# A batched graph layer: sums of two batches turned in one go, the last two products halved, and batches 1 and 2 split into high and low parts like the later ones

## Chip, cores and metric

The kernel runs on one core of one Trainium2 chip. The metric is the device time of one execution in microseconds (us). Before the change three runs took 205.3, 205.43 and 205.56 us, median 205.43. The profiled execution took 205.48 us; its span, from the first to the last instruction, is 203.7 us.

## What is computed

For each of 16 batches with 512 nodes and 128 features:

```
h    = relu(layernorm(x))                         # 512 x 128
A    = [adj, adj, S, adj^T, adj^T, S^T, I]        # 7 relations; S is I shifted by one row
HW_r = h @ W[r, :128] + W_edges[r] @ W[r, 128:]   # the second term is one row per relation
out  = x + max over r of (A_r @ HW_r) + b
```

The relations with adj and adj^T (two each) need `adj @ h` and `adj^T @ h`, called g and gT here, and the row sums of adj and adj^T for the edge term. The other three work on h itself.

## The kernel before, in words

Everything is kept transposed, 128 features by 512 nodes. The batches go through one after another, numbered 0 to 15, in a pipeline over the engines. The order on each engine is written out by hand, and semaphores tie the engines together. There is no planner.

TensorE (PE) does for a batch: `aggregate_T` (bank_gT = gT), `turn_h` (four transposes of h), `aggregate` (bank_g), `turn_sums` (four 128x128 products that turn the row sums into rows, `bank_s`), products 0 to 2 on hT, `begin_products` (four 32-row products that start the banks of products 3 to 6 with the edge term from `c_rows` and `sumsT`), and products 3 to 6 on gT and g. A product is three passes (L870 to L872), since numbers are kept as a high part in fp32r and a low part that holds the rest: high by high, low by high, high by low. From batch 2 (`FIRST`) on, the aggregations take such parts too: `a_hi`, `a_lo` of adj, `aT_hi`, `aT_lo` of its transpose, `h_hi`, `h_lo` of h, four chunks of 128 nodes each, so 12 matmuls per aggregation. Batches 0 and 1 are aggregated whole, in plain fp32 (L763, L770, L780, L789), and batch 2 half and half.

ScalarE (ACT) makes the high parts with the row sums as a by-product (`split_adj` L422, `split_adjT` L431; for batches 0 and 1 it forms the sums alone, L403, L411, L505, L512), the standard deviation (`std_of` L395), h and h_hi (`make_h` L443, L449), the high parts of hT, gT and g (L455, L461, L467), `sumsT` (L473), and starts the running maximum with product 0 (`begin_best` L480).

VectorE (DVE) makes mean and variance (`variance` L550, L557), turns them into scale and shift (`scale_and_shift` L587, L589), makes the low parts of the first two chunks (`split_adj_lo` L596, `split_adjT_lo` L603) and of h, hT, gT, g, and takes the maximum over products 1 to 6 (`take_best` L637, L640).

GpSimd (POOL) makes the low parts of the last two chunks (L334, L341), spreads the sums into `sum_parts` (`part_sums` L307, L311), starts the DMA that adds x onto the bias (`add_bias` L319), and adds it to the maximum (`finish` L327). SyncE (SP) issues the loads and stores (L231 adj, L244 adjT, L250 bias, L254 store, L289 last store).

Which work depends on which, around the change: h of batch b+1 needs scale and shift, these need `std_of`, which needs `variance`. Product 0 of a batch needs the low part of hT, so it waits for ACT (L455), then DVE (L614). The last product of batch 15 is computed in two halves of 256 nodes, each with its own bank, maximum, sum and store.

Of the kernel before, what the change touches and what calls it, by code (L numbers as in the profile page):

```python
# [11 lines left out]
P = 128  # L12
# [14 lines left out]
FIRST = 2  # L27
NX = 4


def gnn_kernel(nc: bass.Bass, x: bass.AP, xT: bass.AP, adj: bass.AP, adjT: bass.AP, W: bass.AP,
# [14 lines left out]
    with ExitStack() as ctx:  # L46
# [26 lines left out]
        summed = pair("summed", [P, 2, C, N], mybir.dt.bfloat16)  # L73
# [5 lines left out]
        g_lo = sb("g_lo", [P, N], F32R)  # L79

# [43 lines left out]
        last_banks = (bank_g, bank_p[0])  # L124
# [66 lines left out]
        best_done = sem("best_done")  # L191
        xb_in = [sem(f"xb_in{i}") for i in range(2)]
# [15 lines left out]

        block = ctx.enter_context(nc.Block())

        @block.sync
        def _(sp):
# [7 lines left out]
            def load_adj(b):  # L220
                q = b % 2
                if b >= 2:
                    if b - 2 < FIRST:
                        sp.wait_ge(sums_ready, 2 * (b - 2) + 1)
# [4 lines left out]
                if b > 2 + FIRST:  # L229
                    sp.wait_ge(alo_last_ready, (b - 2 - FIRST) * NG)  # L230
                sp.dma_start(adj_sb[q][:, :, :], adj_dram[b]).then_inc(adj_in[q], 16)  # L231

            def load_adjT(b):
                q = b % 2
                if b >= 2:
                    if b - 2 < FIRST:
                        sp.wait_ge(sums_ready, 2 * (b - 2) + 2)
# [30 lines left out]
            sp.dma_start(w_sb[:, 5:7, :], w_dram[:, 0:2, :]).then_inc(wa_in, 16)  # L268
            load_adj(1)
            load_adjT(1)  # L270
            load_x(2)
            load_bias(0)
            load_x(3)
            load_adj(2)
            load_adjT(2)
            load_bias(1)
            for b in range(1, B):
                if b + 3 < B:
                    load_x(b + 3)
# [15 lines left out]
        def _(pool):  # L295
            def part_sums(b):
                q = b % 2
# [6 lines left out]
                if b >= 2:  # L304
                    pool.wait_ge(sumsT_psum, b - 1)
                for copy in range(2):
                    last = nc.gpsimd.tensor_copy(sum_parts[q][:, :, :, :, 2 * copy], s)  # L307
                last.then_inc(parts_hi, 1)
                pool.wait_ge(parts_hi, b + 1)
                for copy in range(2):  # L310
                    last = nc.gpsimd.tensor_tensor(sum_parts[q][:, :, :, :, 2 * copy + 1], s,  # L311
                                                   sum_parts[q][:, :, :, :, 2 * copy].bitcast(F32), ALU.subtract)
# [57 lines left out]
            add_bias(0)  # L370
            part_sums(1)
            finish(0)
            add_bias(1)
            part_sums(2)
            add_bias(2)
            for b in range(2, B):

                pool.wait_ge(aTlo_ready, (b - FIRST + 1) * ND)
                finish(b - 1)
                if b + 1 < B:  # L380

# [4 lines left out]
                    part_sums(b + 1)  # L386
                    add_bias(b + 1)

        @block.scalar
        def _(act):  # L390
# [8 lines left out]
            def sum_adj(b):  # L399
                q = b % 2  # L400
                act.wait_ge(adj_in[q], times(b))
                for c in range(C):
                    last = nc.scalar.activation(summed[q][:, 0, c, :], adj_sb[q][:, c, :], ACT.Copy,  # L403
                                                accum_out=sums[q][:, 0, c:c + 1])
                last.then_inc(sums_ready, 1)

            def sum_adjT(b):
                q = b % 2
                act.wait_ge(adjT_in[q], times(b))
                for c in range(C):  # L410
                    last = nc.scalar.activation(summed[q][:, 1, c, :], adjT_sb[q][:, c, :], ACT.Copy,  # L411
                                                accum_out=sums[q][:, 1, c:c + 1])
                last.then_inc(sums_ready, 1)

            def split_adj(b):
# [4 lines left out]
                act.wait_ge(parts_lo, b - 1)  # L420
                for c in range(C):
# [12 lines left out]
            def make_h(b):  # L434
# [10 lines left out]
                last.then_inc(h_ready, 1)  # L445
                if b < FIRST:
                    return
                act.wait_ge(h_ready, b + 1)
# [20 lines left out]
            def copy_sumsT(b):  # L469
                act.wait_ge(sumsT_psum, b + 1)  # L470
# [32 lines left out]
            for c in range(C):  # L503
                act.wait_ge(adj0_in[c], 16)
                last = nc.scalar.activation(summed[0][:, 0, c, :], adj_sb[0][:, c, :], ACT.Copy,  # L505
# [4 lines left out]
            for c in range(C):  # L510
                act.wait_ge(adjT0_in[c], 16)
                last = nc.scalar.activation(summed[0][:, 1, c, :], adjT_sb[0][:, c, :], ACT.Copy,  # L512
# [4 lines left out]
            make_h(1)  # L517
            copy_sumsT(0)
            act.wait_ge(ccol_ready, 1)
            begin_best(0)  # L520
            sum_adj(1)
            std_of(2)
            sum_adjT(1)
            for b in range(1, B):

                if 2 <= b < B - 1:
                    split_adj(b + 1)
                split_gT(b)
# [15 lines left out]
        def _(dve):  # L544
# [82 lines left out]
            def take_best(b, i):  # L627
                q = b % 2
                r = ORDER[i]
                if i == 1:  # L630
                    dve.wait_ge(best_begun, b + 1)
                else:
                    dve.wait_ge(best_done, b * NBEST + i - 1)
                dve.wait_ge(prod_psum, b * NPROD + i + 1)
                product = bank_of[i][:, 0:N]
# [10 lines left out]
            nc.vector.tensor_reduce(row_hi[:, :], groups[:, :, 0:2], AXIS.XY, ALU.add)  # L646
            nc.vector.tensor_reduce(row_lo[:, :], groups[:, :, 2:4], AXIS.XY, ALU.add).then_inc(masks_ready, 1)
# [15 lines left out]
            for i, rels in enumerate((A_RELS, AT_RELS)):  # L663
# [29 lines left out]
            scale_and_shift(2)

            split_gT_lo(1)
            split_hT_lo(1)
            split_h_lo(2)
            split_g_lo(1)
            variance(3)
            take_best(1, 1)  # L700
            take_best(1, 2)
            split_adj_lo(2)
            scale_and_shift(3)
            for i in range(NH, NPROD):
                take_best(1, i)

            for b in range(2, B):
                if b + 2 < B:
                    variance(b + 2)
                split_adjT_lo(b)  # L710
                split_gT_lo(b)
                split_hT_lo(b)
                if b + 2 < B:
                    scale_and_shift(b + 2)
                if b + 1 < B:
                    split_adj_lo(b + 1)
# [8 lines left out]
            dve.wait_ge(best_done, B * NBEST - 1)  # L725
            for i, nodes in enumerate(HALVES):
                dve.wait_ge(prod_psum, B * NPROD + i)
                nc.vector.tensor_tensor(best[q][:, nodes], last_banks[i][:, nodes], best[q][:, nodes],
                                        ALU.max).then_inc(best_done, 1)
                dve.wait_ge(best_done, B * NBEST + i)  # L730
                nc.vector.tensor_tensor(o_sb[q][:, nodes], best[q][:, nodes], x_bias[q][:, nodes],
                                        ALU.add).then_inc(last_out_ready, 1)

        @block.tensor
        def _(pe):
# [8 lines left out]
            def turn_sums(b):  # L744
                pe.wait_ge(parts_lo, b + 1)
                if b >= 1:
                    pe.wait_ge(best_done, (b - 1) * NBEST + 2)
                for c in range(C):
                    last = nc.tensor.matmul(bank_s[:, c * P:(c + 1) * P],  # L749
                                            sum_parts[b % 2][:, c, :, :, :].rearrange("p d g k -> p (d g k)"),  # L750
# [212 lines left out]
```

## Time and profile before

| | us |
|---|---|
| time of three runs, median | 205.43 |
| time of the profiled execution | 205.48 |
| its span | 203.7 |
| PE busy | 197.7 (97%) |
| VectorE busy | 170.0 (83%) |
| ScalarE busy | 160.1 (79%) |
| GpSimd busy | 115.8 (57%) |

The time of the execution is 1.8 us above its span, which is start and end outside the instructions. The chain that ended last is made of the pieces of work that each released the next; where one engine makes up nearly all of it, the others only count where they make that engine wait. A line such as `50.09 1.64 ACT L443 ACTIVATE h<-x_sb x4` says that four instructions of line 443 ran from 50.09 us for 1.64 us; a bracket behind it says how long the engine was idle before and what ended that.

### The profile page before, as it was taken

The numbers are of one execution on the slowest core, as the hardware profiler recorded it, in microseconds if no ns is written. First come the engines' busy times: TensorE is split into PE (matmuls) and PEld (weight loads), VectorE is DVE, ScalarE is ACT, GpSimd is POOL, SyncE is SP. The second block draws the span as 40 slices with busy tenths as digits, with TensorE's granted clock in tenths as the row PEclk, the third lists the DMA queues.
The fourth block names the chain that finished last, engine by engine and source line by source line (L and its number), as shares of the span: only waits on it lengthen the run. The fifth ranks groups of instructions, "written<-read, shape, count | busy, mean of one in ns | idle before, by whom it ended". The sixth has DMA issues, their size and how long they took to land.

```text
span 203.7 us, 3448 instructions
## 1 busy us (share of the span) xinstructions
PE 197.7 (97%) x918; PEld 151.2 (74%) x918; DVE 170.0 (83%) x411; ACT 160.1 (79%) x432; POOL 115.8 (57%) x162
## 2 busy tenths in 40 slices
PE   6999999999999999999999999999999999999991
PEld 6456466778787787878778787878878787887871
DVE  3487969989898998989989898998989899878565
ACT  3887989996969879696988969697896969795230
POOL 4041341477574938657592956759295675939500
PEclk9999999999999999999999999999999999999999
DMA  5999999997888979789987969799795969570501
GB/s 161 333 356 358 373 346 273 293 357 191 258 315 232 350 183 342 201 269 306 292 304 162 381 153 333 228 246 357 198 395 107 312 199 343 208 154 0 100 4 51
DMA packets 33748, 51.07 MB, mean 251 GB/s; under 512 B 1873, under 2 KB 11329, under 8 KB 33729
## 3 DMA queue, kind: packets, MB, share of 16 engines
q1 hardware_dynamic: 31152, 46.53, 67.1%
q0 software_dynamic: 2304, 4.20, 13.3%
q8 instruction: 7, 0.11, 0.2%
q10 hardware_dynamic: 272, 0.13, 0.2%
q14 instruction: 13, 0.10, 0.1%
HBM read 46.65 MB, written 4.19 MB: 250 GB/s over the span
## 4 chain that ended last, share of the span: by engine, by line
PE 94%; DMA 2%; DVE 2%; SPq 0%; issue 0%; DVEq 0%
PE bank_p L870 13%; PE bank_p L871 11%; PE bank_p L872 10%; PE bank_g L832 6%; PE bank_g L835 6%; PE bank_g L841 6%; PE bank_gT L818 6%; PE bank_gT L812 6%; PE bank_gT L808 6%; PE bank_p L741 3%; PE bank_p L860 3%; PE bank_p L749 3%; DMA adj_sb<-in_adj_dram 2%; PE bank_g L789 2%; PE bank_gT L780 2%; PE bank_g L770 2%
## 5 line engine op out<-in xcount | busy, mean ns | idle before, releaser
L334 POOL TENSOR_TENSOR a_lo<-adj_sb,a_hi 128x512 fp32r<-128x512 f32 x26 | 33.1, 1296 | 31.6 <-DVE a_lo L596 28.5
L640 DVE TENSOR_TENSOR best<-bank_p,best 128x512 f32<-128x512 f32 x48 | 33.1, 691 | 7.2 <-PE bank_p L872 6.0
L422 ACT ACTIVATE a_hi<-adj_sb 128x512 fp32r<-128x512 f32 x56 | 34.5, 620 | 1.3 <-DMA adj_sb<-in_adj_dram 1.3
L431 ACT ACTIVATE aT_hi<-adjT_sb 128x512 fp32r<-128x512 f32 x56 | 34.4, 620 | 0.0
L341 POOL TENSOR_TENSOR aT_lo<-adjT_sb,aT_hi 128x512 fp32r<-128x512 f32 x26 | 33.2, 1297 | 0.9 <-ACT aT_hi L431 0.3
L327 POOL TENSOR_TENSOR o_sb<-best,x_bias 128x512 f32<-128x512 f32 x15 | 19.8, 1317 | 19.1 <-DVE aT_lo L603 15.9
L637 DVE SCALAR_TENSOR_TENSOR best<-bank_p,c_col,best 128x512 f32<-128x512 f32 x32 | 24.0, 750 | 6.6 <-ACT best L480 6.0
L461 ACT ACTIVATE gT_hi<-bank_gT 128x512 fp32r<-128x512 f32 x16 | 9.5, 595 | 25.0 <-PE bank_gT L818 24.7
L443 ACT ACTIVATE h<-x_sb,shift,rstd 128x128 f32<-128x128 f32 x60 | 24.7, 488 | 0.0
L870 PE MATMUL bank_p<-hT_hi,w_hi 128*128 128x512 f32 x48 | 20.0, 417 | 0.0
L872 PE MATMUL bank_p<-hT_lo,w_hi 128*128 128x512 f32 x48 | 18.7, 390 | 0.0
L871 PE MATMUL bank_p<-hT_hi,w_lo 128*128 128x512 f32 x48 | 18.7, 389 | 0.0
L596 DVE TENSOR_TENSOR a_lo<-adj_sb,a_hi 128x512 fp32r<-128x512 f32 x28 | 18.0, 683 | 0.0
L603 DVE TENSOR_TENSOR aT_lo<-adjT_sb,aT_hi 128x512 fp32r<-128x512 f32 x28 | 17.9, 681 | 0.0
L319 POOL DMA_DIRECT2D x_bias<-in_xT_dram x16 | 13.8, 863 | 5.0 <-DMA x_bias<-in_biasT_dram 4.6
L832 PE MATMUL bank_g<-aT_hi,h_hi 128*128 128x512 f32 x54 | 16.3, 422 | 0.0
L808 PE MATMUL bank_gT<-a_hi,h_hi 128*128 128x512 f32 x54 | 14.9, 397 | 0.0
L835 PE MATMUL bank_g<-aT_hi,h_lo 128*128 128x512 f32 x54 | 14.7, 392 | 0.0
L841 PE MATMUL bank_g<-aT_lo,h_hi 128*128 128x512 f32 x54 | 14.6, 390 | 0.0
L818 PE MATMUL bank_gT<-a_lo,h_hi 128*128 128x512 f32 x54 | 14.6, 390 | 0.0
L812 PE MATMUL bank_gT<-a_hi,h_lo 128*128 128x512 f32 x54 | 14.5, 389 | 0.0
L619 DVE TENSOR_TENSOR gT_lo<-bank_gT,gT_hi 128x512 fp32r<-128x512 f32 x16 | 11.1, 691 | 3.8 <-ACT gT_hi L461 2.8
(122 smaller groups left out, 477.7 us busy)
## 6 DMA issues: line engine op xcount, KB each, us to landing
adj_sb<-in_adj_dram SPq DMA_DIRECT2D x15, 1024.0 KB, 7.5
adjT_sb<-in_adjT_dram SPq DMA_DIRECT2D x15, 1024.0 KB, 8.3
x_bias<-in_biasT_dram SPq DMA_DIRECT2D x16, 256.0 KB, 6.5
x_bias<-in_xT_dram POOLq DMA_DIRECT2D x16, 256.0 KB, 4.1
x_sb<-in_x_dram SPq DMA_DIRECT2D x15, 256.0 KB, 8.3
out_dram<-o_sb SPq DMA_DIRECT2D x15, 256.0 KB, 5.5
adj_sb<-in_adj_dram SPq DMA_DIRECT2D x4, 256.0 KB, 5.1
adjT_sb<-in_adjT_dram SPq DMA_DIRECT2D x4, 256.0 KB, 5.1
```

The costliest lines, as they stand in the source:

```text
L334: nc.gpsimd.tensor_tensor(a_lo[q][:, c, :], adj_sb[q][:, c, :], a_hi[q][:, c, :].bitcast(F32), ALU.subtract).then_inc(alo_last_ready, 1)
L341: nc.gpsimd.tensor_tensor(aT_lo[q][:, c, :], adjT_sb[q][:, c, :], aT_hi[q][:, c, :].bitcast(F32), ALU.subtract).then_inc(aTlo_last_ready, 1)
L422: nc.scalar.activation(a_hi[q][:, c, :], adj_sb[q][:, c, :], ACT.Copy, accum_out=sums[q][:, 0, c:c + 1]).then_inc(ahi_ready, 1)
L431: nc.scalar.activation(aT_hi[q][:, c, :], adjT_sb[q][:, c, :], ACT.Copy, accum_out=sums[q][:, 1, c:c + 1]).then_inc(aThi_ready, 1)
L640: op = nc.vector.tensor_tensor(best[q][:, :], product, best[q][:, :], ALU.max)
L808: nc.tensor.matmul(bank_gT[:, 0:N], h_hi[q][:, c, :], a_hi[q][:, c, :], start=(c == 0 and b > FIRST), stop=False)
L818: last = nc.tensor.matmul(bank_gT[:, 0:N], h_hi[q][:, c, :], a_lo[q][:, c, :], start=False, stop=(c == split_chunks(b)[-1]))
L832: nc.tensor.matmul(bank_g[:, 0:N], h_hi[q][:, c, :], aT_hi[q][:, c, :], start=(c == 0 and b > FIRST), stop=False)
L835: nc.tensor.matmul(bank_g[:, 0:N], h_lo[q][:, c, :], aT_hi[q][:, c, :], start=False, stop=False)
L870: nc.tensor.matmul(dst, w_hi[:, i, :], hi[:, nodes], start=start, stop=False)
L871: nc.tensor.matmul(dst, w_lo[:, i, :], hi[:, nodes], start=False, stop=False)
L872: return nc.tensor.matmul(dst, w_hi[:, i, :], lo[:, nodes], start=False, stop=stop)
```

## The change

In batches 4 to 15 the row sums of two neighbours go through one `turn_sums` and one `copy_sumsT`. The even one of a pair (`leads`) does it, with the sums of the odd one (`follows`) in other columns of the same `sum_parts`, and `c_rows` has a second set of rows that picks them. For that, ACT splits all of the odd batch's adj and adjT before it takes gT of the even one, and SP loads adjT ahead of the store. The last two products of batch 15, not one, are halved, and POOL adds x and bias of the first half. `FIRST` is 1: batch 1 is split like the later ones and batch 2 in all chunks. The first bias is loaded ahead of adj of batch 1, the second ahead of adj of batch 2. The order on ACT, DVE and POOL for batches 0 to 4 is written out anew.

```diff
-FIRST = 2
+FIRST = 1
+PAIRED = 4
+        def leads(b):
+            return b >= PAIRED and (b - PAIRED) % 2 == 0 and b + 1 < B
+        def follows(b):
+            return b >= 1 and leads(b - 1)
+        def turn_of(b):
+            return b if b < PAIRED else PAIRED + (b - PAIRED) // 2
...
+            load_bias(0)
             load_adj(1)
             load_adjT(1)
             load_x(2)
-            load_bias(0)
+            load_bias(1)
+            load_adj(2)
             load_x(3)
-            load_adj(2)
             load_adjT(2)
-            load_bias(1)
...
                 if b + 2 < B:
                     load_adj(b + 2)
+                    load_adjT(b + 2)
                 store(b - 1)
...
             add_bias(0)
+            pool.wait_ge(alo_ready, ND)
+            pool.wait_ge(hlo_ready, 1)
+            split_adj_last(1)
             part_sums(1)
+            pool.wait_ge(aTlo_ready, ND)
+            split_adjT_last(1)
+            add_bias(1)
             finish(0)
...
                 finish(b - 1)
+                if leads(b):
+                    part_sums(b + 1)
                 if b + 1 < B:
                     pool.wait_ge(alo_ready, (b - FIRST + 2) * ND)
                     pool.wait_ge(hlo_ready, b - FIRST + 2)
                     split_adj_last(b + 1)
                     split_adjT_last(b + 1)
-                    part_sums(b + 1)
+                    if not leads(b):
+                        part_sums(b + 1)
...
-            sum_adj(1)
+            split_adj(1)
+            split_adjT(1)
...
+            begin_best(2)
+            std_of(3)
+            make_h(3)
+            split_h(3)
+            split_adjT(3)
+            std_of(4)
+            for b in range(3, B):
+                if b < B - 1:
                     split_adj(b + 1)
+                if leads(b):
+                    split_adjT(b + 1)
                 split_gT(b)
                 split_hT(b)
...
+            for i in range(NH, NPROD):
+                take_best(2, i, i - 1)
+            variance(4)
+            scale_and_shift(4)
+            for b in range(3, B):
+                split_adjT_lo(b)
...
                 aggregate_T(b)
                 turn_h(b)
                 aggregate(b)
-                turn_sums(b)
+                if not follows(b):
+                    turn_sums(b)
...
-            for nodes, to in zip(HALVES, last_banks):
-                product(B - 1, NPROD - 1, nodes, to)
+            for i in range(2):
+                for k in range(NLAST):
+                    product(B - 1, NPROD - NLAST + k, HALVES[i], last_banks[k][i])
```

On ACT, before the change, this stands from `begin_best` of batch 2 (it writes best0) to `h` of batch 4 (h0, std0 and rstd0 again belong to an even batch, a_hi0 too).

```order
L480 ACTIVATE best0<-bank_p0,c_col 128x512
L431 ACTIVATE aT_hi1,sums1<-adjT_sb1 128x512 x4
L422 ACTIVATE a_hi0,sums0<-adj_sb0 128x512 x4
L461 ACTIVATE gT_hi<-bank_gT 128x512
L455 ACTIVATE hT_hi<-bank_p1 128x512
L395 ACTIVATE std1<-mean_var1,eps 128x4
L443 ACTIVATE h0<-x_sb0,shift0,rstd0 128x128 x4
```

On ACT, with the change, from `begin_best` of batch 2 to `h` of batch 4:

```order
L500 ACTIVATE best0<-bank_p0,c_col 128x512
L427 ACTIVATE std1<-mean_var1,eps 128x4
L460 ACTIVATE h1<-x_sb3,shift1,rstd1 128x128 x4
L469 ACTIVATE h_hi1<-h1 128x512
L448 ACTIVATE aT_hi1,sums1<-adjT_sb1 128x512 x4
L427 ACTIVATE std0<-mean_var0,eps 128x4
L439 ACTIVATE a_hi0,sums0<-adj_sb0 128x512 x4
L481 ACTIVATE gT_hi<-bank_gT 128x512
L475 ACTIVATE hT_hi<-bank_p1 128x512
L460 ACTIVATE h0<-x_sb0,shift0,rstd0 128x128 x4
```

The standard deviation of batch 4 (std0, L427) now stands ahead of the splitting of adj of batch 4 and of gT and hT of batch 3. Before, the one for batch 4 (std0, L395) came after gT and hT of batch 2, and h of batch 3 was made there, ahead of `begin_best` of batch 2.

On DVE, with the change, from the scale of batch 3 (rstd1) to the low part of hT of batch 3; best0 is the maximum of batch 2, mean_var0 and rstd0 are of batch 4:

```order
L635 SCALAR_TENSOR_TENSOR shift1<-mean_var1,rstd1 128x4
L642 TENSOR_TENSOR a_lo1<-adj_sb1,a_hi1 128x512 x2
L695 SCALAR_TENSOR_TENSOR best0<-bank_p1,c_col,best0 128x512
L695 SCALAR_TENSOR_TENSOR best0<-bank_p2,c_col,best0 128x512
L655 TENSOR_TENSOR h_lo1<-h1,h_hi1 128x512
L698 TENSOR_TENSOR best0<-bank_p3,best0 128x512
L698 TENSOR_TENSOR best0<-bank_p4,best0 128x512
L698 TENSOR_TENSOR best0<-bank_p5,best0 128x512
L698 TENSOR_TENSOR best0<-bank_g,best0 128x512
L596 BN_STATS stats<-x_sb0 128x6 x4
L601 MEMSET wait_carrier 128x1
L603 BN_AGGR mean_var0<-stats 128x2 x4
```

On DVE, before the change, the same stretch, from the scale of batch 3 (rstd1, shift1, which stands in the middle of the maxima of batch 1) on:

```order
L589 SCALAR_TENSOR_TENSOR shift1<-mean_var1,rstd1 128x4
L640 TENSOR_TENSOR best1<-bank_p3,best1 128x512
L640 TENSOR_TENSOR best1<-bank_p4,best1 128x512
L640 TENSOR_TENSOR best1<-bank_p5,best1 128x512
L640 TENSOR_TENSOR best1<-bank_g,best1 128x512
L550 BN_STATS stats<-x_sb0 128x6 x4
L555 MEMSET wait_carrier 128x1
L557 BN_AGGR mean_var0<-stats 128x2 x4
L603 TENSOR_TENSOR aT_lo0<-adjT_sb0,aT_hi0 128x512 x2
```

The mean and variance of batch 4 stood behind the maxima of batch 1; they now stand behind those of batch 2, and the scale of batch 3 behind g of batch 2.

## Rows read from the trace of the kernel before

**Rows 1.** The chain that ended last, shares of the span by engine.
```profile
PE 94%; DMA 2%; DVE 2%; SPq 0%; issue 0%; DVEq 0%
```
**Rows 2.** Stretches of batches 1, 2, 3: busy per engine, granted clock, DMA share, GB/s.
```profile
19.98:33.67 13.69, 13.67 (x51) 8.16 (x51) 11.20 (x36) 12.56 (x37) 3.88 (x7) 1.00 1.05 332
33.67:46.17 12.50, 12.50 (x54) 8.66 (x54) 11.76 (x28) 12.47 (x36) 7.31 (x10) 1.00 1.04 327
46.17:57.97 11.80, 11.80 (x59) 9.40 (x58) 10.63 (x26) 9.85 (x28) 8.12 (x11) 1.00 0.84 249
```
**Rows 3.** Chain in order of time: start, us, piece; batches 1 and 3.
```profile
27.75 0.40 PE bank_p L749 x4
...
48.90 0.44 PE bank_p L741 x4
...
52.10 0.40 PE bank_p L749 x4
52.50 0.29 PE bank_p L870
...
54.60 0.43 PE bank_p L860 x3
```
**Rows 4.** Timeline of ACT, batches 0, 1 and 3.
```profile
17.24 0.60 ACT L473 ACTIVATE sumsT<-bank_p 128x512 fp32r<-128x512 f32 x1 [1.02 <-PE bank_p L749]
...
18.30 0.63 ACT L403 ACTIVATE summed<-adj_sb 128x512 bf16<-128x512 f32 x1
...
48.93 0.60 ACT L461 ACTIVATE gT_hi<-bank_gT 128x512 fp32r<-128x512 f32 x1 [1.87 <-PE bank_gT L818]
...
49.90 0.30 ACT L395 ACTIVATE std<-mean_var,eps 128x4 f32<-128x4 f32 x1
50.09 1.64 ACT L443 ACTIVATE h<-x_sb,shift,rstd 128x128 f32<-128x128 f32 x4
...
52.31 0.58 ACT L467 ACTIVATE g_hi<-bank_g 128x512 fp32r<-128x512 f32 x1
...
53.28 0.69 ACT L480 ACTIVATE best<-bank_p,c_col 128x512 f32<-128x512 f32 x1
```
**Rows 5.** Costliest groups: busy, mean ns of one; the splitting of adj on ACT.
```profile
L422 ACT ACTIVATE a_hi<-adj_sb 128x512 fp32r<-128x512 f32 x56 | 34.5, 620 | 1.3 <-DMA adj_sb<-in_adj_dram 1.3
```
**Rows 6.** Timeline of DVE, batches 0 and 3.
```profile
18.45 1.54 DVE L637 SCALAR_TENSOR_TENSOR best<-bank_p,c_col,best 128x512 f32<-128x512 f32 x2 [1.38 <-ACT best L480]
...
47.01 0.86 DVE L550 BATCH_NORM_STATS2 stats<-x_sb 128x6 f32<-128x128 f32 x4
...
48.01 0.28 DVE L557 BATCH_NORM_AGGREGATE mean_var<-stats 128x2 f32<-128x6 f32 x3
...
50.77 0.17 DVE L587 RECIPROCAL rstd<-std 128x4 f32<-128x4 f32 x1
...
51.05 1.28 DVE L596 TENSOR_TENSOR a_lo<-adj_sb,a_hi 128x512 fp32r<-128x512 f32 x2
52.43 0.69 DVE L609 TENSOR_TENSOR h_lo<-h,h_hi 128x512 fp32r<-128x512 f32 x1
...
56.03 2.14 DVE L640 TENSOR_TENSOR best<-bank_p,best 128x512 f32<-128x512 f32 x3 [0.47 <-PE bank_p L872]
```
**Rows 7.** Timeline of POOL, batches 0 and 3.
```profile
20.60 1.00 POOL L319 DMA_DIRECT2D x_bias<-in_xT_dram  x1 [4.60 <-DMA x_bias<-in_biasT_dram]
...
53.26 2.55 POOL L334 TENSOR_TENSOR a_lo<-adj_sb,a_hi 128x512 fp32r<-128x512 f32 x2 [2.40 <-DVE a_lo L596]
```
**Rows 8.** One line, the loads of adjT (L244): landing times.
```profile
DMA to landing us min/median/max: 6.6/8.3/12.3
```
**Rows 9.** Timeline of DVE at the end, batch 15.
```profile
197.52 2.14 DVE L640 TENSOR_TENSOR best<-bank_p,best 128x512 f32<-128x512 f32 x3 [0.48 <-PE bank_p L872]
199.86 0.42 DVE L728 TENSOR_TENSOR best<-bank_g,best 128x256 f32<-128x256 f32 x1 [0.20 <-DVE best L640]
...
201.11 0.42 DVE L731 TENSOR_TENSOR o_sb<-best,x_bias 128x256 f32<-128x256 f32 x1
```

More of the change, by code:

```diff
@@ L20 @@
 NBEST = NPROD - 1
+NLAST = 2
 NH = len(H_RELS)
@@ L303, in part_sums @@
                     pool.wait_ge(aThi_ready, (b - FIRST + 1) * NS)
-                if b >= 2:
-                    pool.wait_ge(sumsT_psum, b - 1)
+                if turn >= 2:
+                    pool.wait_ge(sumsT_psum, turn - 1)
+                parts = sum_parts[turn % 2]
                 for copy in range(2):
-                    last = nc.gpsimd.tensor_copy(sum_parts[q][:, :, :, :, 2 * copy], s)
+                    last = nc.gpsimd.tensor_copy(parts[:, :, :, :, first + 2 * copy], s)
                 last.then_inc(parts_hi, 1)
@@ L310, in part_sums @@
                 for copy in range(2):
-                    last = nc.gpsimd.tensor_tensor(sum_parts[q][:, :, :, :, 2 * copy + 1], s,
-                                                   sum_parts[q][:, :, :, :, 2 * copy].bitcast(F32), ALU.subtract)
+                    last = nc.gpsimd.tensor_tensor(parts[:, :, :, :, first + 2 * copy + 1], s,
+                                                   parts[:, :, :, :, first + 2 * copy].bitcast(F32), ALU.subtract)
                 last.then_inc(parts_lo, 1)
@@ L396, in std_of, with split_adj @@
                                      bias=eps[:, :]).then_inc(std_ready, 1)
[L399 to L415, printed above, removed]
+            def split_adj(b, chunks=range(C)):
                 q = b % 2
@@ L419, in split_adj @@
                     act.wait_ge(gT_psum, b - 1)
-                act.wait_ge(parts_lo, b - 1)
-                for c in range(C):
+                if b >= 2:
+                    act.wait_ge(parts_lo, b - 1)
+                for c in chunks:
                     nc.scalar.activation(a_hi[q][:, c, :], adj_sb[q][:, c, :], ACT.Copy,
@@ L645, in _ @@
             groups = ident[:, :].rearrange("p (g s) -> p g s", s=GROUP)
-            nc.vector.tensor_reduce(row_hi[:, :], groups[:, :, 0:2], AXIS.XY, ALU.add)
-            nc.vector.tensor_reduce(row_lo[:, :], groups[:, :, 2:4], AXIS.XY, ALU.add).then_inc(masks_ready, 1)
+            for s in range(2):
+                nc.vector.tensor_reduce(row_hi[:, s:s + 1], groups[:, :, 4 * s:4 * s + 2], AXIS.XY, ALU.add)
+                last = nc.vector.tensor_reduce(row_lo[:, s:s + 1], groups[:, :, 4 * s + 2:4 * s + 4], AXIS.XY, ALU.add)
+            last.then_inc(masks_ready, 1)
             first_variance(0, half_stats_done, half_aggr_done)
@@ L709, in _ @@
+            variance(4)
+            scale_and_shift(4)
+            for b in range(3, B):
+                split_adjT_lo(b)
+                if 3 < b < B - 2:
                     variance(b + 2)
-                split_adjT_lo(b)
                 split_gT_lo(b)
                 split_hT_lo(b)
+                if b == 3:
+                    variance(b + 2)
+                if b + 1 < B:
+                    split_adj_lo(b + 1)
+                    if not leads(b):
+                        split_h_lo(b + 1)
+                split_g_lo(b)
+                if leads(b):
+                    split_h_lo(b + 1)
+                for i in range(1, NPROD - NLAST * int(b == B - 1)):
+                    take_best(b, i, i - 1)
@@ L918, in _ @@
             for b in range(1, B):
-                if b < FIRST:
-                    aggregate_T_whole(b)
-                else:
-                    aggregate_T(b)
+                aggregate_T(b)
                 turn_h(b)
-                if b < FIRST:
-                    aggregate_whole(b)
-                else:
-                    aggregate(b)
-                turn_sums(b)
+                aggregate(b)
+                if not follows(b):
+                    turn_sums(b)
                 for i in range(NH):
```

267 lines of the change are left out of this document (138 added, 129 removed).

## Prediction

> **What bounds the kernel now.** I read the chain of waits first: PE makes up 94% of it [rows 1], so only time that PE works or is made to wait counts. Then the stretches batch by batch: batch 1, aggregated whole in fp32, takes 13.69 us, batch 2, half whole, 12.50, batch 3 and every later one 11.8; PE is busy in all but 0.02 us of each, at a granted clock of 1.00 [rows 2]. DVE is busy 10.63 us of 11.80, ACT 9.85: PE bounds, with little room on DVE. The chain in order of time gives the parts of a batch. In batch 3, which begins at 46.17, `aggregate_T` ends at 48.90, `turn_sums` runs from 52.10 to 52.50, product 0 starts at 52.50 (6.33 us into the batch), products 0 to 2 last to 54.60, and the edge terms with products 3 to 6 to 57.97 (3.37 us) [rows 2, 3].
>
> **The change part by part.** All sums are made against the profiled execution, 205.48 us, 0.05 above the median of the runs.
>
> *Batches 1 and 2 split.* Ideally they shrink to 11.8 us, by 1.9 and 0.7. Batch 1 does not get its share, for its parts come late. ACT begins to split adj of batch 1 where it now forms its sums, at 18.30, and a chunk takes 0.62, so the second is ready at 19.6 [rows 4, 5]. DVE takes the first maximum from 18.45 (0.77), then two low parts of adj (1.2) and of h (0.7): done at 21.05 [rows 6]. Only then POOL starts its two chunks, 0.14 later (as after h_lo, 52.43 + 0.69 to 53.26), and ends 2.55 later, at 23.7 [rows 6, 7]. PE, ready for the last one at 22.7, ends `aggregate_T` at about 24.1. The same in `aggregate`: DVE takes three more maxima (0.77 + 2 x 0.72) and two low parts, to 24.4, POOL needs 2.55 more, to 27.05, PE ends at about 27.4. Now it ends at 27.75 [rows 3]. So batch 1 gains 0.3, not 1.9. In batch 2 the same sums put each low part 0.5 us or more ahead of its use, and it takes 11.8: another 0.7. Batch 3 then starts at 45.2 instead of 46.17. POOL can begin that early because the first bias is loaded sooner: it now waits 4.60 us for it, to 20.60 [rows 7]. With 256 KB ahead of it, adj of batch 1 lands later, but nothing waited for it at 18.30. The copy of h to h_hi that batch 1 gains hides in the 1.02 us that ACT waits ahead of sumsT [rows 4].
>
> *The new order around batch 3.* This is the costly edit. `std_of(4)` now stands on ACT ahead of the split of adj of batch 4 and of gT and hT of batch 3, and what it waits for, the variance of batch 4, stands on DVE behind the maxima of batch 2. Counted from the start of batch 2 (durations start to start from [rows 4 to 6]): ACT takes gT_hi at 2.76 (48.93 less 46.17), hT_hi, then splits adj of batch 3 (2.45) to 6.2, makes g_hi and sumsT (0.97) and `begin_best` (0.6), to 7.7, and std of batch 3, to 8.0. DVE: scale 0.28, two low parts 1.2, maxima 1 and 2 1.5, h_lo 0.65, maxima 3 to 6 4 x 0.72, variance 1.28: it ends at 15.7, which is 3.9 us into batch 3. Then std (0.3, of which 0.2 before the next can start), split of adj of batch 4 (2.45), gT_hi and hT_hi (0.5 + 0.6) on ACT: 19.4; hT_lo behind gT_lo on DVE: 20.2. Product 0 of batch 3 starts at 20.3, where it would have started at 11.8 + 6.33 = 18.1: PE waits 2.2 us. Behind hT_hi ACT still has h and h_hi of batch 4 (2.2), g_hi (0.5) and sumsT (0.6), to 22.6; product 2, ready at 21.7, waits 0.95 more. On DVE the variance of batch 5, two low parts, h_lo and g_lo (1.2 + 1.2 + 0.6 + 0.7) follow hT_lo and end at 23.85; the edge terms, ready at 23.4, wait 0.55. Sum: 3.7 us. Batch 4 starts 27.4 us after batch 2, at 60.7; before, at 57.97. The two early gains, 1.0, are paid back 3.7-fold. The waits are sure in place and uncertain in size: if PE meets each with 0.1 to 0.2 more delay on resuming, 4.2; if DVE overlaps better than start to start, 3.0.
>
> *Pairs.* Batches 5, 7, 9, 11, 13, 15 lose `turn_sums`: 0.40 us, and perhaps the 0.06 by which the first pass behind it is longer than a usual 0.23 (0.29) [rows 3]. I take 0.43, six times 2.6; bounds 2.4 and 2.8. The six copies of sumsT that ACT drops are off the path. What the pair adds is lateness: ACT splits adj and adjT of the odd batch (4.9 us) ahead of gT_hi of the even one, behind adjT of the even one, and reaches gT_hi 3.5 us into the batch, not 2.76. hT_lo is then ready at 5.4 and needed at 6.33; POOL's parts of the odd batch's sums are ready at 4.6 and needed at 5.9; g_lo at 7.3, needed at 8.4. So the cover is 0.9 us, and behind that each tenth of lateness costs PE a tenth per pair.
>
> *The end.* Since DVE bounds it, the maxima count: now three whole ones from 197.52, then two half maxima and two half sums, the last ending at 201.53, 4.01 us [rows 9]. With the change two whole ones (1.44), then half maxima of products 5 and 6, twice, and one half sum; POOL adds the other. With 0.45 for a half that waits for the one before and 0.34 for one that doesn't, this is 1.45 + 0.45 + 0.34 + 0.45 + 0.45 + 0.42 = 3.56: 0.45 less. POOL's half sum, estimated at half of its 1.3 us, ends at 3.1, before DVE's.
>
> Sum: -0.3 - 0.7 + 3.7 - 2.6 - 0.45 = -0.35; with PE's slower resuming I take -0.3, so 205.2 us.
>
> **The rivals.**
> 1. *The wait in batch 3 doesn't come, or half of it.* For it: DVE has idle time, and the maxima of batch 2 end about 1 us into batch 3 today (47.01 starts the variance) [rows 6]. Against it: DVE can't start them before std of batch 3, which is behind `begin_best`. Without the 3.7, the time is 201.5; with half, 203.3.
> 2. *The load of the odd adjT is late (slower).* It is issued when POOL has made the low parts of the odd batch before, about 13.5 us into a pair, and ACT wants it at 24.2: 10.7 us. Landing took 8.3 us in the median and 12.3 at worst [rows 8]. From 11.6 us on the 0.9 us of cover is gone; at 12.3, 1.6 us late, hT_lo costs PE 0.8 us in five pairs: 205.2 + 4 = 209.2. Against it: the long landings fall in the first 30 us, where the DMA share is above 1.00, and 0.84 is usual later [rows 2].
> 3. *DVE becomes the bound in the odd batches.* It works 10.63 us [rows 2] and waits 0.47 for product 3 [rows 6]; at 11.4 us a batch some 0.3 is left. If it doesn't go below 11.8, the pairs bring nothing: 207.8.
> 4. *PE's clock falls in the wait of batch 3.* The granted clock is 1.00, the level of 2.4 GHz, in every stretch above, where PE never pauses [rows 2]; no row shows it after a pause of 2.2 us. The 5.5 us of products left in batch 3 at half the clock, 1.2 GHz, less 1.5 of waiting that they would hide, add 4: 209.2. [...]
>
> **How the numbers follow.** Forecast 62%, 205.2, its own range 204.4 to 206.2; rival 1 23% (half of that below 203); rival 2 7%; rival 3 5%; rival 4 3%. A measurement of this kernel can tell 0.2%, 0.41 us, from no change. The forecast lies 0.23 below the median, within that bound: of its 62% I give 24 to faster (below 205.02), 28 to the same, 10 to slower (above 205.84). With rival 1 faster has 47%, the same 28%, and slower, with rivals 2 to 4, 25%. The range, 202.9 to 206.8, leaves out the lower half of rival 1 and most of rivals 2 to 4.
>
> **What would show it.** Right: batch 3 lasts 15 to 16 us, with PE waiting ahead of product 0 for hT_lo, and ACT idle about 2.5 us ahead of the std of batch 4, released by the variance; batch 1 some 13.4; later even batches 11.8, odd ones 11.4; no `turn_sums` in these. Wrong: batch 4 starting before 58 us (rival 1), gT_hi of even batches released by adjT's DMA (rival 2), odd batches of 11.8 with maxima as the last to end (rival 3), a granted clock below 1.00 in batch 3 (rival 4).

## The result and the profile after

The changed kernel takes 209.13 us (median of four runs, 208.81 to 209.53), the kernel before in the same comparison 205.50: a ratio of 1.0168, 95% interval 1.0143 to 1.0193. It is slower by about 3.5 us, where 205.2 was forecast and 206.8 was the upper end of the range. The profiled execution took 208.81 us, its span is 207.0, 3.3 above that of before. Ratios leave out runs over 1.5% above the fastest of the same kernel (one of e4 below, two of e8, 206.3 to 207.5 us); medians keep them.

The stretches of batches 1 to 5 answer to [rows 2] (from, to, length, busy time and count of PE, PEld, DVE, ACT, POOL, then granted clock, DMA share, GB/s):

```profile
19.96:34.24 14.28, 12.80 (x61) 9.32 (x58) 12.76 (x28) 12.08 (x34) 10.80 (x12) 1.00 1.08 346
34.24:46.95 12.71, 12.36 (x59) 9.35 (x57) 11.65 (x27) 10.23 (x28) 6.88 (x9) 1.00 0.90 293
46.95:62.72 15.77, 14.42 (x59) 10.49 (x58) 13.82 (x37) 13.29 (x40) 13.00 (x14) 0.89 0.77 234
62.72:75.15 12.43, 12.04 (x59) 9.32 (x57) 10.70 (x26) 10.68 (x31) 9.54 (x14) 1.00 0.84 253
75.15:86.50 11.35, 11.35 (x55) 8.95 (x54) 10.77 (x26) 8.32 (x23) 7.89 (x8) 1.00 0.87 263
```

PE, busy all the time before, now waits in batches 1 to 4 and 12. The six odd batches from 5 on are 0.44 us shorter each, as forecast; batch 3 is 3.97 longer (forecast 3.7). By the first matmul of each batch, batch 2 starts at 34.24 instead of 33.51 and batch 3 at 46.95 instead of 46.01 (the stretches of [rows 2] are cut 0.16 later). So batch 1 costs 0.7 more where 0.3 less was forecast, batch 2 0.2 more where 0.7 less was, and batches 4 and 12, forecast unchanged, are longer by 0.64 and 0.45. PE's timeline names the main waits (not shown are 0.71 us for POOL's a_lo in batch 1, which was forecast, and 0.35 for DVE's aT_lo in batch 3):

```profile
28.04 0.49 PE L892 MATMUL bank_g<-aT_lo,h_hi 128*128 128x512 f32 x1 [0.74 <-POOL aT_lo L355]
...
38.21 1.20 PE L884 MATMUL bank_g<-aT_hi,h_hi 128*128 128x512 f32 x4 [0.23 <-DVE best L698]
...
55.61 0.73 PE L922 MATMUL bank_p<-hT_hi,w_hi 128*128 128x512 f32 x1 [0.83 <-issue]
...
69.17 0.66 PE L833 MATMUL bank_p<-ident_r,sum_parts 128*128 128x128 f32 x4 [0.39 <-POOL sum_parts L325]
...
162.20 0.66 PE L833 MATMUL bank_p<-ident_r,sum_parts 128*128 128x128 f32 x4 [0.20 <-POOL sum_parts L325]
```

Three of the five lead to POOL. The wait of batch 3 that is put down to "issue" ends right behind DVE's hT_lo (55.51), as predicted. On ACT, too, batch 3 looks as predicted: std of batch 4 waits 2.45 us for the variance, and gT_hi starts 6.67 us into the batch, where it started 2.92 into it before (48.93 less 46.01). DVE's line first, then two of ACT:

```profile
54.83 0.68 DVE L660 TENSOR_TENSOR hT_lo<-bank_p,hT_hi 128x512 fp32r<-128x512 f32 x1
```
```profile
50.96 0.30 ACT L427 ACTIVATE std<-mean_var,eps 128x4 f32<-128x4 f32 x1 [2.45 <-DVE mean_var L603]
...
53.62 0.58 ACT L481 ACTIVATE gT_hi<-bank_gT 128x512 fp32r<-128x512 f32 x1
```

How long POOL and DVE took in batches 1 and 2 was in no step of the prediction. First POOL, then DVE (start, duration of the group):

```profile
21.20 2.54 POOL L348 TENSOR_TENSOR a_lo<-adj_sb,a_hi 128x512 fp32r<-128x512 f32 x2 [4.23 <-DVE h_lo L655]
23.69 1.27 POOL L321 CAST sum_parts<-sums 128x16 fp32r<-128x16 f32 x2
25.05 0.45 POOL L325 TENSOR_TENSOR sum_parts<-sums,sum_parts 128x16 fp32r<-128x16 f32 x2
25.44 2.55 POOL L355 TENSOR_TENSOR aT_lo<-adjT_sb,aT_hi 128x512 fp32r<-128x512 f32 x2
...
32.27 2.56 POOL L348 TENSOR_TENSOR a_lo<-adj_sb,a_hi 128x512 fp32r<-128x512 f32 x2 [2.16 <-DVE a_lo L642]
```
```profile
23.08 1.81 DVE L649 TENSOR_TENSOR aT_lo<-adjT_sb,aT_hi 128x512 fp32r<-128x512 f32 x2
24.82 1.41 DVE L698 TENSOR_TENSOR best<-bank_p,best 128x512 f32<-128x512 f32 x2
...
33.56 1.82 DVE L655 TENSOR_TENSOR h_lo<-h,h_hi 128x512 fp32r<-128x512 f32 x1
```

Where POOL works and DVE has an operation with two inputs in SBUF, one or both get long: DVE's aT_lo 1.81 us for two, where a_lo of the same size took 1.28, h_lo 1.82 instead of 0.69 [rows 6], POOL's CAST 1.27 for two instead of 0.34 (the line of e2 below). A maximum, which reads one input from PSUM, keeps its 0.7. The delay shows as duration of the instruction, not as idle time with a releaser.

### The profile page after: what moved, and what is told of

The parts are those of the page before. It is cut to its first block and busy times, and to the rows that moved or that the text cites. A ratio compares the mean times of both kernels' runs of the same rounds, so it can differ in the third digit from the quotient of the medians.

```text
span 207.0 us, 3419 instructions
## 1 busy us (share of the span) xinstructions
PE 196.9 (95%) x910; PEld 151.1 (73%) x910; DVE 177.5 (86%) x420; ACT 157.5 (76%) x427; POOL 134.7 (65%) x171
## 5 line engine op out<-in xcount | busy, mean ns | idle before, releaser
L348 POOL TENSOR_TENSOR a_lo<-adj_sb,a_hi 128x512 fp32r<-128x512 f32 x30 | 38.3, 1298 | 46.2 <-DVE a_lo L642 19.4
L355 POOL TENSOR_TENSOR aT_lo<-adjT_sb,aT_hi 128x512 fp32r<-128x512 f32 x30 | 38.3, 1300 | 0.4 <-ACT aT_hi L448 0.4
L439 ACT ACTIVATE a_hi<-adj_sb 128x512 fp32r<-128x512 f32 x60 | 37.0, 628 | 0.0
L448 ACT ACTIVATE aT_hi<-adjT_sb 128x512 fp32r<-128x512 f32 x60 | 37.0, 626 | 0.0
L341 POOL TENSOR_TENSOR o_sb<-best,x_bias 128x512 f32<-128x512 f32 x15 | 21.9, 1457 | 3.1 <-DVE aT_lo L649 3.1
L649 DVE TENSOR_TENSOR aT_lo<-adjT_sb,aT_hi 128x512 fp32r<-128x512 f32 x30 | 20.8, 732 | 0.0
L892 PE MATMUL bank_g<-aT_lo,h_hi 128*128 128x512 f32 x60 | 16.8, 397 | 1.2 <-POOL aT_lo L355 0.7
L873 PE MATMUL bank_gT<-a_lo,h_hi 128*128 128x512 f32 x60 | 16.6, 394 | 0.8 <-POOL a_lo L348 0.7
L867 PE MATMUL bank_gT<-a_hi,h_lo 128*128 128x512 f32 x60 | 16.2, 391 | 0.1
L325 POOL TENSOR_TENSOR sum_parts<-sums,sum_parts 128x16 fp32r<-128x16 f32 x32 | 14.5, 475 | 1.3
```

The costliest lines, as they stand in the source:

```text
L341: nc.gpsimd.tensor_tensor(o_sb[q][:, :], best[q][:, :], x_bias[q][:, :], ALU.add).then_inc(out_ready, 1)
L348: nc.gpsimd.tensor_tensor(a_lo[q][:, c, :], adj_sb[q][:, c, :], a_hi[q][:, c, :].bitcast(F32), ALU.subtract).then_inc(alo_last_ready, 1)
L355: nc.gpsimd.tensor_tensor(aT_lo[q][:, c, :], adjT_sb[q][:, c, :], aT_hi[q][:, c, :].bitcast(F32), ALU.subtract).then_inc(aTlo_last_ready, 1)
L439: nc.scalar.activation(a_hi[q][:, c, :], adj_sb[q][:, c, :], ACT.Copy, accum_out=sums[q][:, 0, c:c + 1]).then_inc(ahi_ready, 1)
L448: nc.scalar.activation(aT_hi[q][:, c, :], adjT_sb[q][:, c, :], ACT.Copy, accum_out=sums[q][:, 1, c:c + 1]).then_inc(aThi_ready, 1)
L649: nc.vector.tensor_tensor(aT_lo[q][:, c, :], adjT_sb[q][:, c, :], aT_hi[q][:, c, :].bitcast(F32), ALU.subtract).then_inc(aTlo_ready, 1)
```

## Experiments

The theory from these rows had two parts: in batch 3 the order (std behind a late variance), everywhere else POOL and DVE holding each other up. The rivals were that such instructions were long for reasons of their own, and that PE's clock made batch 3 long. Ratios are to the kernel before in the same comparison.

**e1: std of batch 4 early.** On ACT (first cut) its std moves up, on DVE (the other two) its variance, from behind the maxima of batch 2.
```diff
             split_h(3)
+            std_of(4)
             split_adjT(3)
-            std_of(4)
...
             scale_and_shift(3)
+            variance(4)
             split_adj_lo(3)
...
                 take_best(2, i, i - 1)
-            variance(4)
             scale_and_shift(4)
```


> The changed kernel, but ACT takes the std of batch 4 behind h_hi of batch 3, ahead of the split of adjT of batch 3, and DVE takes the variance of batch 4 behind the scale of batch 3, ahead of the low parts and maxima of batch 2. Order theory (batch 3 lost 4.0 us because ACT waited 2.45 us for the variance behind six maxima): batch 3 lasts 12.0 to 12.8 us instead of 15.8, the granted clock stays at 1.00 in it, the time is 205.3 to 206.2. Rival (the loss in batch 3 is mainly PE's clock or work of POOL and DVE that hold each other up, and the wait only stands beside it): batch 3 stays at 14 us or more, the time above 207.5.

Measured: 210.60 us, 1.0243 (1.0208 to 1.0278); slower still, batch 3 at 17.65. ACT's wait for the variance is gone, and the time is not. PE now waits for g_lo, at the end of a stretch (43 to 59 us) in which DVE has no pause. DVE, POOL and PE in that batch, and PE's clock behind the wait (from, to, length, busy time of PE, PEld, DVE, ACT, POOL, then granted clock, DMA share, GB/s):

```profile
50.84 1.03 DVE L635 SCALAR_TENSOR_TENSOR shift<-mean_var,rstd 128x4 f32<-128x4 f32 x1
51.79 2.38 DVE L649 TENSOR_TENSOR aT_lo<-adjT_sb,aT_hi 128x512 fp32r<-128x512 f32 x2
...
56.48 1.70 DVE L642 TENSOR_TENSOR a_lo<-adj_sb,a_hi 128x512 fp32r<-128x512 f32 x2
```
```profile
50.57 3.05 POOL L355 TENSOR_TENSOR aT_lo<-adjT_sb,aT_hi 128x512 fp32r<-128x512 f32 x2
```
```profile
59.53 0.50 PE L912 MATMUL bank_p<-sumsT,c_rows 32*128 32x512 f32 x3 [1.77 <-DVE g_lo L670]
```
```profile
62.00:63.00 1.00, 1.00 (x4) 0.81 (x3) 0.41 (x2) 1.00 (x5) 1.00 (x2) 0.50 1.09 358
```

Earlier work of DVE falls on POOL's: shift, four numbers per lane, takes 1.03 instead of 0.16; the three lines are 2.4 us longer than alone. Behind the wait the clock fell to 0.50, and products 3 to 6 took 4.46 us (59.96 to 64.42) instead of 2.86 in the changed kernel (59.86 to 62.72). So 1.6 us of this batch are the clock's; the run of e1 with a mean clock of 0.997 still took 210.09. The order theory by itself fell; the rival named both POOL and DVE and the clock, and both had a part.

**e2: POOL to be kept off DVE's aT_lo in batch 1 and h_lo in batch 2.**
```diff
       split_adj_last(1)
-      part_sums(1)
       pool.wait_ge(aTlo_ready, ND)
       split_adjT_last(1)
+      part_sums(1)
...
       pool.wait_ge(alo_ready, 2 * ND)
+      pool.wait_ge(hlo_ready, 2)
       split_adj_last(2)
```


> The changed kernel, but POOL starts its half of aT_lo of batch 1 only when DVE has ended its own (part_sums of batch 1 behind it), and its half of a_lo of batch 2 only when DVE has ended h_lo. Theory that POOL and DVE hold each other up where DVE reads two tiles of SBUF (h_lo 1.82 us instead of 0.69, POOL's copies of the sums 1.27 for a pair instead of 0.44): DVE's two aT_lo of batch 1 take 1.3 us together instead of 1.8, h_lo of batch 2 takes 0.7, batch 1 gets shorter by 0.1 to 0.7 us and batch 2 by 0.2 to 0.6; the time is 207.6 to 208.6. Rival (these instructions are slow for a reason of their own, as a late operand): the durations stay, each added wait makes POOL later, and the time is 208.9 to 209.8.

Measured: 210.27 us, 1.0213 (1.0165 to 1.0261): no gain. h_lo, now apart, is back at 0.68, and POOL's casts of batch 1, now behind aT_lo, at 0.34 (the 0.44 of the expectation is the pair behind them). In batch 2 POOL, later by that, meets DVE's next one instead, at 2.7 times its length:

```profile
33.73 0.68 DVE L656 TENSOR_TENSOR h_lo<-h,h_hi 128x512 fp32r<-128x512 f32 x1
...
37.11 3.48 DVE L650 TENSOR_TENSOR aT_lo<-adjT_sb,aT_hi 128x512 fp32r<-128x512 f32 x2
```
```profile
27.53 0.34 POOL L321 CAST sum_parts<-sums 128x16 fp32r<-128x16 f32 x2
...
37.04 3.00 POOL L355 TENSOR_TENSOR aT_lo<-adjT_sb,aT_hi 128x512 fp32r<-128x512 f32 x2
```

DVE's aT_lo of batch 1 stayed at 1.81, as POOL's a_lo reaches into it up to 23.80. PE's wait for POOL's aT_lo there fell from 0.74 to 0.33, but it now waits 0.30 for the parts of the sums. The durations follow the overlap, as the theory says; its forecast of the time was wrong, since a wait at one place moves the overlap, or the lateness, to another.

**e6: the old kernel, with the two waits taken away that hold POOL back.** The sharpest test, as nothing else changes.
```diff
-      pool.wait_ge(alo_ready, (b - FIRST + 2) * ND)
-      pool.wait_ge(hlo_ready, b - FIRST + 2)
       split_adj_last(b + 1)
```


> The kernel before, in which POOL no longer waits for DVE's a_lo and h_lo ahead of its own half of a_lo, so that it starts up to 2.4 us earlier, right behind the sum that ends a batch. The data it needs are there by then. Theory that POOL and DVE hold each other up when DVE reads two tiles of SBUF: DVE's two a_lo and h_lo, 1.28 and 0.69 us before, take 2.0 or more and 1.2 or more, g_lo comes later than PE needs it, a batch lasts 12.2 to 13.8 us instead of 11.8, the time is 211 to 230 although nothing was added. Rival (a wait taken away costs nothing): batches of 11.8, time 204.5 to 206.

Measured, in two runs: 222.14 us, 1.0807 (1.0770 to 1.0844). DVE in batch 7, POOL beside it, and PE:

```profile
105.23 1.16 DVE L587 SCALAR_TENSOR_TENSOR shift<-mean_var,rstd 128x4 f32<-128x4 f32 x1
106.32 2.38 DVE L594 TENSOR_TENSOR a_lo<-adj_sb,a_hi 128x512 fp32r<-128x512 f32 x2
108.62 0.68 DVE L607 TENSOR_TENSOR h_lo<-h,h_hi 128x512 fp32r<-128x512 f32 x1
109.22 0.68 DVE L622 TENSOR_TENSOR g_lo<-bank_g,g_hi 128x512 fp32r<-128x512 f32 x1
```
```profile
105.08 3.06 POOL L334 TENSOR_TENSOR a_lo<-adj_sb,a_hi 128x512 fp32r<-128x512 f32 x2
```
```profile
110.04 0.50 PE L858 MATMUL bank_p<-sumsT,c_rows 32*128 32x512 f32 x3 [1.19 <-DVE g_lo L622]
```

Two operations of DVE take 3.54 us instead of 1.44, POOL's pair 3.06 instead of 2.55, and PE waits 1.19 us for g_lo in every batch of 3 to 13, which last 13.06 us. Only h_lo, expected long, escaped: POOL's pair had ended by then (108.14). That POOL waits 2.40 us in [rows 7] was no slack: the wait kept it off DVE. The Trainium skill (SBUF — State Buffer, "Who interferes with whom") says that a DVE instruction with two SBUF inputs contends with a GpSimd instruction that reads SBUF, and that a DVE instruction with at most one, outside DVE's faster two-port modes, does not. The rows of shift and a_lo agree with the first, the maxima beside POOL in batch 1 above (1.41 us for two) with the second.

**e5: e1 with less work of POOL.** POOL leaves out its two chunks of aT_lo of batch 3.
```diff
+      if b == 3:
+          nc.gpsimd.memset(spare[:, c:c + 1], 0.0).then_inc(aTlo_last_ready, 1)
+          continue
```


> The kernel of e1 (std of batch 4 early), in which POOL leaves out its two chunks of aT_lo of batch 3, so that these low parts are not computed and batch 3 comes out with old ones. In e1 DVE's two aT_lo of batch 3 took 2.38 us instead of 1.28, beside POOL's 3.05 instead of 2.5. Theory that the two hold each other up, and that this is what ate the gain of e1: DVE's pair takes 1.3 us, its shift, a_lo and g_lo come 1.5 to 2.5 us earlier, PE's wait of 1.77 us for g_lo shrinks to under 0.7, PE's clock stays at 1.00 in batch 3, which lasts 12.0 to 14.0 us instead of 17.65; time 205.8 to 208.0. Rival (DVE is simply behind with its work in batch 3, and POOL has no part in it): DVE's pair stays at 2.4, batch 3 at 16.5 or more, time 209.5 or more.

Measured: 207.85 us, 1.0108 (1.0087 to 1.0128), 2.75 less than e1. DVE's rows are short again, and PE's wait for g_lo falls from 1.77 to 0.31:

```profile
51.68 0.16 DVE L639 SCALAR_TENSOR_TENSOR shift<-mean_var,rstd 128x4 f32<-128x4 f32 x1
51.76 1.33 DVE L653 TENSOR_TENSOR aT_lo<-adjT_sb,aT_hi 128x512 fp32r<-128x512 f32 x2
```

Batch 3 lasts 13.73, within what the theory expected, and PE's clock stays at 1.00: of the 3.9 us by which it is shorter than in e1, 1.6 are the clock's. The other 1.9 us above 11.8 were not taken apart; PE still waits 0.75 for POOL's a_lo, and DVE is busy 7.84 of the 8 us from 46 to 54.

**e3: no pairs.**
```diff
-PAIRED = 4
+PAIRED = 16
```


> The changed kernel without pairs: every batch sums and turns its own parts. If a pair is worth the 0.43 us that an odd batch was seen to be shorter, and the longer batches 4 and 12 (0.64 and 0.45 us) come from POOL's parts of a pair being late, then six pairs brought 2.65 and gave back 1.1: the time is 210.3 to 211.0, every batch from 4 on 11.8 us. Rival (batches 4 and 12 were longer because of what batch 3 left behind, and not because of the pairs): 211.5 to 212.0, with batch 4 still above 12.2 us.

Measured: 210.33 us, 1.0223 (1.0206 to 1.0240): 1.2 more than with pairs. Every batch from 4 to 14 lasts 11.8 us, so batches 4 and 12 were longer because of the pairs. The trace also settles what the clock did in batch 3. Here PE has the waits of the changed kernel (0.78 us ahead of product 0), the clock stays at 1.00, and batch 3 lasts 15.60 instead of 15.77 us. PE's other two waits, for sumsT and g_lo, are the ones that the prediction had:

```profile
47.30:62.90 15.60, 13.20 (x59) 9.29 (x57) 13.89 (x37) 13.11 (x39) 12.59 (x14) 1.00 0.80 238
```
```profile
58.24 0.50 PE L922 MATMUL bank_p<-hT_hi,w_hi 128*128 128x512 f32 x1 [0.66 <-ACT sumsT L493]
...
59.58 0.51 PE L912 MATMUL bank_p<-sumsT,c_rows 32*128 32x512 f32 x3 [0.38 <-DVE g_lo L670]
```

**e9: parts of the odd batch first.**
```diff
+      if leads(b):
+          part_sums(b + 1)
       finish(b - 1)
-      if leads(b):
-          part_sums(b + 1)
```


> The changed kernel, in which POOL makes the parts of the odd batch's sums ahead of the sum that ends the batch before, as in e7. Theory that batches 4 and 12 were longer (0.64 and 0.45 us) because these parts were late: no wait of PE for the parts is left, and if the sum of 1.57 us that then stands beside DVE's a_lo costs nothing, the time is 207.8 to 208.4. Rival (the sum now holds up a_lo, which goes on to g_lo, due 1.0 us later): PE waits 0.2 to 0.8 us for g_lo in most lead batches, and the time is 209 to 212.

Measured: 207.66 us, 1.0102 (1.0083 to 1.0122). No wait for the parts is left, batches 4 and 12 last 11.80. The sum does make a_lo longer (1.77 instead of 1.36 in batch 8), but g_lo still comes in time. Against e3 the pairs are now worth 2.67 us (2.5 by the ratios); 2.6 was forecast. What keeps it 2.0 us above before lies in batches 1 to 3, batch 3 with 15.75 us above all.

**e4, e8: the old start with pairs and halved last products.** e8 is the same kernel again. Against the kernel before (three places of a long edit):
```diff
+NLAST = 2
...
 FIRST = 2
 NX = 4
+PAIRED = 4
...
                 finish(b - 1)
+                if leads(b):
+                    part_sums(b + 1)
```


> The kernel before (batch 1 aggregated whole, batch 2 half whole, its order of work up to batch 3) with the pairs and the halved last products alone. If the loss lies in the first four batches and the rest is worth what the even and odd batches showed: 205.5 less 2.65 less 0.1, and with waits for the parts of a pair in one or two lead batches at most 1.1 back: 202.6 to 203.9. Rival (the pairs cost more in the order of before, where the variance stands ahead of the low parts on DVE, or the start of after helped by the 1.0 us that was forecast): 204.3 or more.

> The kernel of e4 once more beside e7, for its spread and a second profile. If the race for POOL and DVE makes the spread: a profile of a longer run shows PE waiting 0.2 to 0.6 us for the parts of the sums in some lead batches, and long copies of the sums there; medians 203.5 to 204.8. Rival: a longer run shows no such wait, and the difference lies in the first four batches or in the loads.

Measured: 204.39 us, 0.9936 (0.9907 to 0.9965), and 204.30, 0.9930 (0.9900 to 0.9959): by the ratios about 4.8 below the changed kernel and 1.4 below the one before. e4's median is above the 202.6 to 203.9 expected, at the lower edge of its rival. The runs behind these ratios spread from 203.1 to 205.7, all runs to 207.5. Neither profile names a wait for the parts, but in both batch 14 lasts 12.07 instead of 11.8, and PE starts its `turn_sums` 0.06 us behind the end of the parts. That is the same in both; they differ by 0.81 us, and e8's starts batch 1 at 20.47, e4's at 19.63, as the rival had expected.

**e7, e10: two races less.** e7 is e4 with the parts first, as in e9; e10 adds the bias of batch 2 behind the sum that ends batch 1.


> The kernel of e4 (old start, pairs, halved last products), in which POOL makes the parts of the odd batch's sums ahead of the sum that ends the batch before, not behind it. In e4 these parts were ready 0.3 us ahead of PE's turn and lay against DVE's shift and a_lo. Theory that the spread of e4 (203.2 to 205.7) comes from this race: no run waits for the parts, the spread shrinks to under 1 us, the time is 203.0 to 204.0. Rival (the spread comes from elsewhere, or the longer sum, 1.29 us, now meets DVE's a_lo and costs more): the spread stays, the median 204.2 or more.

```diff
       part_sums(2)
-      add_bias(2)
...
       finish(b - 1)
+      if b == 2:
+          add_bias(2)
```


> The kernel of e7, in which POOL adds the bias of batch 2 behind the sum that ends batch 1, not ahead of it. In the profile of e7 POOL waited 3.14 us for that bias to land, so that the sum fell on DVE's a_lo (3.11 us instead of 1.28) and PE waited 0.92 us for g_lo in batch 3. Theory: the sum now starts at DVE's end of aT_lo, batch 3 lasts 11.8 us in every run, the time is 202.9 to 203.5 with a spread under 0.6. Rival (something else delayed batch 3 in that run): medians as e7, 203.4, with a run of 204 or more.

Measured: e7 203.41 us, 0.9900 (0.9882 to 0.9919), 203.15 to 204.20; e10 203.44, 0.9904 (0.9867 to 0.9941), 202.71 to 205.31. The spread of e7 is 1.05 us, just over the 1 us expected. e7's profile is its longest run, and shows the price of one collision. POOL waited for a bias, so that the issue of a DMA and the sum behind it met DVE's a_lo:

```profile
50.87 0.88 POOL L339 DMA_DIRECT2D x_bias<-in_xT_dram  x1 [3.14 <-DMA x_bias<-in_biasT_dram]
51.48 1.59 POOL L347 TENSOR_TENSOR o_sb<-best,x_bias 128x512 f32<-128x512 f32 x1
```
```profile
51.12 3.11 DVE L636 TENSOR_TENSOR a_lo<-adj_sb,a_hi 128x512 fp32r<-128x512 f32 x2
```

1.83 us more on DVE became a wait of 0.92 on PE. In the profile of e10 batch 3 lasts 11.81, but the spread did not shrink, so the theory of the spread is only half borne out: its profile starts batch 1 at 20.40, and what made its run of 205.3 is open. e7 and e10 beat both kernels, the one before by about 2.0 us. e9 and e7, both with the parts first, differ by 4.25 us (4.15 by the ratios): that is the new start and its order, where 2.7 were forecast (-0.3, -0.7 and +3.7).

## Why the prediction was wrong

**Failed: "Batches 1 and 2 split".** The sums let POOL begin behind DVE and gave each low part the duration of the old trace, and "the same sums put each low part 0.5 us or more ahead of its use". In batch 1 POOL would have begun aT_lo at 24.4 and ended at 27.05. It began at 25.44, behind a DVE pair of 1.81 and its own CAST of 1.27, and PE waited 0.74. (The sum had left out POOL's work on the row sums; at 0.34 and 0.45 us it would have been done by about 24.5.) In batch 2 h_lo of 1.82 made PE's second pass and then the maxima late. Up to the start of batch 3 the change was to gain 1.0 and lost 0.94. e2 and e6 show that the long operations follow the overlap of POOL and DVE; that they cost these 1.9 us is read from the order in the trace, and no run won the time back with the new start.

**Failed: the cover of the pairs.** "POOL's parts of the odd batch's sums are ready at 4.6 and needed at 5.9" had the same hole: their second pair took 1.20 us in batch 4 and 0.98 in batch 12, beside a_lo, and PE waited 0.39 and 0.20. In batches 6, 8, 10 and 14 it took 0.45 or less, and PE did not wait. Batches 4 and 12 lost 1.09 together; e3 and e9 show it. The 0.43 per pair itself was right.

**Right: batch 3.** 3.7 forecast, 3.97 measured (3.8 in e3, at a full clock), with ACT's wait and PE's three waits where they were put. Product 0 began 8.66 us into the batch, 8.5 was forecast; the waits for sumsT and g_lo, seen in e3, are 0.66 and 0.38, where 0.95 and 0.55 were. What the sum did not say is what stands behind that wait: e1 took it away and gained nothing, for DVE, 10.63 us busy of 11.80 in [rows 2], then had no pause left, its work fell on POOL's, and the clock fell behind PE's wait.

**Too large: the end.** 0.45 forecast, about 0.1 measured. From its third maximum to its last sum DVE takes 204.65 less 200.91, 3.74 us, not 3.56 (4.01 before): the 0.2 us of waiting ahead of the first half, in [rows 9] too, was left out. And the last store lands 2.35 us behind that, not 2.2.

```profile
200.91 1.42 DVE L698 TENSOR_TENSOR best<-bank_p,best 128x512 f32<-128x512 f32 x2 [0.47 <-PE bank_p L924]
202.52 0.42 DVE L808 TENSOR_TENSOR best<-bank_p,best 128x256 f32<-128x256 f32 x1 [0.20 <-DVE best L698]
...
204.23 0.42 DVE L815 TENSOR_TENSOR o_sb<-best,x_bias 128x256 f32<-128x256 f32 x1
```

The misses are 1.03 (to the start of batch 2), 0.91, 0.27, 1.09 and 0.35 us: 3.65, the distance from 205.2 to the profiled 208.81 but for rounding.

**Rivals.** 1 to 3 did not come. Of rival 4 the event came, not the price: behind a pause of 0.83 us the granted clock fell from 1.00 (2.4 GHz) to 0.50 (1.2 GHz).

```profile
54.00:55.00 1.00, 0.79 (x6) 0.60 (x4) 0.78 (x2) 1.00 (x4) 1.00 (x2) 1.00 0.28 107
55.00:56.00 1.00, 0.39 (x1) 0.42 (x2) 1.00 (x4) 1.00 (x4) 1.00 (x1) 0.83 0.70 221
56.00:57.00 1.00, 1.00 (x4) 0.72 (x4) 0.96 (x8) 0.97 (x3) 0.06 (x1) 0.50 0.85 309
...
59.00:60.00 1.00, 1.00 (x7) 0.37 (x7) 0.96 (x3) 1.00 (x5) 1.00 (x2) 0.97 1.06 193
```

Products 0 to 2 ran at 0.43 us a pass instead of 0.23, but g_lo was ready only at 59.10, and PE came to it at 59.43: about 0.3 us. Against e3, whose batch 3 kept its clock, it is 0.2. In e1 the clock fell while products 3 to 6 ran, which wait for no other engine there, and cost 1.6.

Nor does a pause alone bring the clock down. e3 has nearly the same pause as the changed kernel (0.78 us) and stays at 1.00. In e6 PE waits 1.78 us in batch 2, as long as in e1 (1.77), and again 1.19 us in each of batches 3 to 13, and its clock stays at 1.00 from there to the end of batch 14, also in a stretch in which PE does nothing:

```profile
43.00:44.00 1.00, 0.00 (x0) 0.00 (x0) 1.00 (x3) 1.00 (x4) 0.00 (x0) 1.00 0.95 332
...
45.00:46.00 1.00, 1.00 (x8) 0.69 (x5) 0.96 (x2) 0.94 (x3) 1.00 (x2) 1.00 1.01 368
```

So the clock fell behind some pauses and not behind others of the same length; what decides it is open.

## What to carry to other kernels

Before moving work between VectorE and GpSimd, list for each operation where its inputs lie, and look for pairs that the old order kept apart: a wait that looks like slack can be what keeps two engines off each other, and in e6 its removal cost 17 us. Sum a new order not with durations from a trace in which the neighbours never met, but with both, alone and beside them. And where a moved wait yields nothing, look whether the engine behind it has any pause left.

## What was not expected of the hardware

An operation of DVE with two SBUF inputs that begins beside a POOL operation is not slowed by a share, but held for up to the length of POOL's instruction: four numbers per lane took 1.03 us (e1) and 1.16 us (e6) instead of 0.16, and h_lo of batch 2, begun at 33.56, ended 0.55 us behind POOL's a_lo (34.83). In e7 the issue of a DMA and the sum behind it on POOL (50.87 to 53.07) made two a_lo 1.83 us longer. It works both ways: POOL's small casts took 1.27 us for two instead of 0.34. Neither engine shows as idle meanwhile.
